# Inverse columns with weights of 128 rows by 64 columns, and ten transfers issued from three engines

## What is computed

```python
def _spectral_conv(x, w):
    B, Cin, H, W = x.shape
    x_ft = jnp.fft.rfft2(x, norm='ortho')
    out = jnp.einsum('bixy,ioxy->boxy', x_ft[:, :, :M1, :M2], w.astype(x_ft.dtype))
    out_ft = jnp.zeros((B, w.shape[1], H, W // 2 + 1), dtype=x_ft.dtype)
    out_ft = out_ft.at[:, :, :M1, :M2].set(out)
    return jnp.fft.irfft2(out_ft, s=(H, W), norm='ortho')
...
for sw, cw, cb in ((sw0, cw0, cb0), (sw1, cw1, cb1), (sw2, cw2, cb2), (sw3, cw3, cb3)):
    x1 = _spectral_conv(x, sw)
    x2 = jnp.einsum('bchw,oc->bohw', x, cw) + cb[None, :, None, None]
    x = _gelu(x1 + x2)
```

## Time and profile before

| | |
|---|---|
| median of the runs | 1113.42 us |
| profiled execution, its own time | 1119.4 us |
| its span, first to last instruction | 1117.5 us |
| TensorE busy | 1026.7 us, 92% |
| VectorE, ScalarE, GpSimd busy | 55%, 37%, 12% |
| mean granted TensorE clock | 0.975 of 2.4 GHz |
| inverse columns (L1296), 4096 matmuls | 267.6 us busy |
| inverse rows (L1264), idle until the first modes have landed | 6.9 us, 8 times |

### The profile page before, as it was taken

How to read it: one execution, slowest core, us unless ns; L and a number is a source line. 1 busy time by engine, 2 the same in 40 slices (tenths; PEclk the granted TensorE clock), 3 DMA queues, 4 the chain that set the end, 5 groups by cost and what they waited for, 6 DMA issues and landing times.

```text
span 1117.5 us, 36304 instructions
## 1 busy us (share of the span) xinstructions
PE 1026.7 (92%) x16860; PEld 655.4 (59%) x16860; DVE 618.3 (55%) x773; ACT 410.1 (37%) x554; POOL 137.2 (12%) x127
## 2 busy tenths in 40 slices
PE   4899999999989999999899899999999999689996
PEld 3577667667757633676577567667316788522221
DVE  2257457726833221477358347733153577769887
ACT  2332223223223486232232233223676777411100
POOL 6000000000000000000000000020010755334421
PEclk9999999999999999999999999999999899779999
DMA  5220130022022300310220130020001000000000
GB/s 189 90 75 4 47 100 22 4 90 75 4 76 73 94 6 21 111 41 3 90 76 3 53 96 21 3 91 17 4 22 43 2 2 1 1 1 1 1 10 10
DMA packets 25660, 46.75 MB, mean 42 GB/s; under 512 B 9437, under 2 KB 10488, under 8 KB 24869
## 3 DMA queue, kind: packets, MB, share of 16 engines
q1 hardware_dynamic: 24694, 43.49, 12.6%
q10 hardware_dynamic: 384, 0.66, 0.2%
q0 software_dynamic: 432, 0.29, 0.1%
HBM read 30.25 MB, written 10.89 MB: 37 GB/s over the span
## 4 chain that ended last, share of the span: by engine, by line
PE 73%; DVE 11%; issue 5%; ACT 4%; DMA 3%; SPq 2%; POOL 2%; ACTq 0%; POOLq 0%; DVEq 0%
PE PSALL L1296 23%; PE PSALL L1264 7%; PE PSALL L1159 5%; PE PSALL L1374 4%; PE PSALL L1287 4%; PE PSALL L1173 4%; PE PSALL L525 4%; PE PSALL L1240 3%; PE PSALL L1384 3%; DVE WORK L1504 3%; PE PSALL L428 3%; DMA WORK<-MIXED 2%; PE PSALL L513 2%; DVE WORK L1523 2%; PE PSALL L407 2%
## 5 line engine op out<-in xcount | busy, mean ns | idle before, releaser
L1523 DVE STREAM_TRANSPOSE WORK<-PSALL 128x1024 f32<-128x1024 f32 x128 | 152.4, 1229 | 277.4 <-PE PSALL L1264 277.4
L1296 PEld LDWEIGHTS PSALL<-EW,WORK 64*128 64x128 f32 x4096 | 251.2, 193 | 65.5 <-issue 48.3
L1296 PE MATMUL PSALL<-EW,WORK 64*128 64x128 f32 x4096 | 267.6, 284 | 12.8 <-DVE WORK L1523 12.8
L1424 ACT ACTIVATE X<-PSALL,TABLES 128x1024 f32<-128x1024 f32 x128 | 141.7, 1114 | 336.7 <-PE PSALL L1296 336.7
L1504 DVE STREAM_TRANSPOSE WORK<-PSALL 128x1024 f32<-128x1024 f32 x84 | 104.3, 1241 | 32.8 <-PE PSALL L1159 30.9
L1405 ACT COPY SPEC<-PSALL 128x400 f32<-128x400 f32 x64 | 54.0, 850 | 136.8 <-PE PSALL L1173 132.8
L1173 PEld LDWEIGHTS PSALL<-TABLES,WORK 128*64 128x64 f32 x2000 | 67.1, 138 | 48.6 <-DVE WORK L1504 31.4
L705 POOL MEMSET SW<- 64x4160 f32 x1 | 3.6, 3560 | 712.6 <-PE PSALL L1248 712.6
L1004 DVE TENSOR_TENSOR WORK<-PSALL,X 128x832 f32<-128x832 f32 x80 | 79.8, 1018 | 19.4 <-PE PSALL L513 17.9
L1173 PE MATMUL PSALL<-TABLES,WORK 128*64 128x64 f32 x2000 | 80.7, 228 | 7.8 <-DVE WORK L1504 3.8
L525 PE MATMUL PSALL<-WORK,SPEC 128*64 128x416 f32 x320 | 74.8, 549 | 0.0
(11 more groups left out here) (157 smaller groups left out, 1166.6 us busy)
## 6 DMA issues: line engine op xcount, KB each, us to landing
SW<-in_spec_w SPq DMA_DIRECT2D x160, 80.0 KB, 2.5
spec_scr<-MIXED SPq DMA_DIRECT2D x24, 400.0 KB, 3.3
SPEC<-spec_scr SPq DMA_DIRECT2D x32, 200.0 KB
WORK<-spec_scr SPq DMA_DIRECT2D x16, 200.0 KB
WORK<-MIXED SPq DMA_DIRECT2D x64, 40.0 KB
WORK<-in_coords_w SPq DMA_DIRECT2D x2, 1024.0 KB, 4.8
XC<-in_coords_c SPq DMA_DIRECT2D x2, 1024.0 KB, 7.2
hid_scr<-WORK SPq DMA_DIRECT2D x64, 8.0 KB
```

What stands on the lines that cost most here:

```text
L1296: m = pe.matmul(PS[2 * p + z][:, 2 * b * GRID:(2 * b + 2) * GRID], G[64 * z:64 * z + 64, n % 2, b, h:h + 4, :, c].rearrange("p q o -> p (q ...
L1424: nc.scalar.activation(X[:, n].rearrange("p b (z d) c w -> p d z b (c w)", z=2)[:, p, :, :, 2 * t * GRID:2 * (t + 1) * GRID], PSALL[:, 2 * ...
L1523: nc.vector.transpose(G[:, n % 2, 2 * x + y].rearrange("p h o v -> p o h v"), PSALL[:, 4 + 2 * x:6 + 2 * x, :].rearrange("p k (h o v) -> p ...
```

## The change

In `image_columns` one product now has 128 rows of G by 64 columns as weights; the two column tiles j (`tile_position` (0, 0) and (0, 64)) write the two halves of the partitions of one bank. EW becomes a block-diagonal table of 128 rows by 128 columns: the upper 64 rows hold the transform for the first 64 output columns and the lower ones for the other 64. So one product covers both c, and each region of PSUM is added to once instead of twice. The number of products, and the 128 columns that each streams, stay. The tables of the inverse rows are put into another order to match. The ten transfers are shared out anew: SyncE issues x = 0 of d = 0 to 3 and x = 1 of d = 4, ScalarE x = 0 of d = 4, and GpSimd x = 1 of d = 0 to 3 with a counter of its own, for which TensorE and VectorE wait too. `keep_busy` is called with 2 instead of 3.

```diff
         DW = sb("DW", [128, 2, 2 * Q])
-        EW = sb("EW", [128, 3 * GRID])
+        EW = sb("EW", [128, 2 * GRID])
         ident = sb("ident", [128, 128])
...
         stored = [Count(sem(f"modes_stored{g}"), 1, unit=16) for g in range(NG)]
-        straight_in = Count(sem("first_modes_copied"), 1, unit=16 * 2 * KXD)
+        straight_in = Count(sem("first_modes_copied"), 1, unit=16 * (KXD + 1))
+        pool_straight_in = Count(sem("first_modes_copied_by_pool"), 1, unit=16 * (KXD - 1))
         loaded = [None] + [Count(sem(f"modes_loaded{g}"), 1, unit=32) for g in range(1, NG)]
...
-        def straight(eng, d, x):
+        def straight(eng, d, x, count):
...
                           MIXED[NG * x:128:2 * NG, d * MODES * CH:(d + 1) * MODES * CH]
-                          ).then_inc(straight_in.sem, 16)
+                          ).then_inc(count.sem, 16)
...
                     turn.wait(mix_ready, -(-(d + 1) * KYG // 4))
-                    for x in range(2):
-                        straight(sp, d, x)
+                    straight(sp, d, 0, straight_in)
                 turn.wait(mix_ready, N_MIX)
+                straight(sp, KXD - 1, 1, straight_in)
                 for n in range(1, NG):
...
                     turn.wait(straight_in, 1)
+                    turn.wait(pool_straight_in, 1)
                 elif y == 0:
...
-                for c in range(2):
-                    h = 4 * (2 * p + t)
-                    for z in range(2):
-                        m = pe.matmul(PS[2 * p + z][:, 2 * b * GRID:(2 * b + 2) * GRID],
-                                      G[64 * z:64 * z + 64, n % 2, b, h:h + 4, :, c].rearrange("p q o -> p (q o)"),
-                                      EW[64 * z:64 * z + 64, (1 - c) * GRID:(3 - c) * GRID],
-                                      start=False, stop=True, skip_group_check=True, tile_position=(64 * z, 0))
+                for z in range(2):
+                    for j in range(2):
+                        h = 4 * (2 * z + p) + 2 * j
+                        m = pe.matmul(PS[2 * p + z][64 * j:64 * j + 64, 2 * b * GRID:(2 * b + 2) * GRID],
+                                      G[:, n % 2, b, h:h + 2, :, t].rearrange("p q o -> p (q o)"), EW[:],
+                                      start=False, stop=True, skip_group_check=True, tile_position=(0, 64 * j))
                 return m
...
                 pointwise(l, 0, 0)
-                keep_busy(3)
+                keep_busy(2)
                 inverse_rows(l, 0, 0)
...
                     act.wait_ge(ho_out.sem, p * ho_out.stride)
-                for x in range(2):
-                    straight(act, KXD - 1, x)
+                straight(act, KXD - 1, 0, straight_in)
...
                         turn.wait(straight_in, 1)
+                        turn.wait(pool_straight_in, 1)
                         for g in range(1, NG):
...
                 pool.dma_start(dst[:], src).then_inc(tail_w, 16)
+
+            turn = Steps(pool)
+            for p in range(PASSES):
+                for l in range(LAYERS):
+                    if l == 0 and p:
+                        pool.wait_ge(ho_out.sem, p * ho_out.stride)
+                    for d in range(KXD - 1):
+                        turn.wait(mix_ready, -(-(d + 1) * KYG // 4))
+                        straight(pool, d, 1, pool_straight_in)
+                    turn.next()
             tail_pool(pool)
...
     twice = np.where(k == 0, 1.0, 2.0)[:, None]
-    idft_w = np.zeros((2, RI, Q, GRID))
-    idft_w[:, 0, 0:MODES], idft_w[:, 1, 0:MODES] = twice * cos.T, -twice * sin.T
+    idft_w = np.zeros((2, RI, Q, 2, GRID))
+    for c in range(2):
+        idft_w[c, 0, 0:MODES, c], idft_w[c, 1, 0:MODES, c] = twice * cos.T, -twice * sin.T
...
         forward = np.array(forward).reshape(2, Q)
-        inverse = [row_of(l, 2 * half + p, q, 2 * t + c)
-                   for half in range(2) for p in range(2) for t in range(SETS) for q in range(4) for c in range(2)]
+        inverse = [row_of(l, p, q, 2 * t + c)
+                   for c in range(2) for p in range(4) for q in range(4) for t in range(SETS)]
         inverse = np.array(inverse).reshape(2, Q)
...
         "outside": 1 - band, "band4": np.tile(band * f(HD ** -0.5), (1, 4)),
-        "idft_w": np.pad(idft_w.reshape(128, GRID), ((0, 0), (GRID, GRID))).astype(f), "ident": np.eye(128, dtype=f),
+        "idft_w": idft_w.reshape(128, 2 * GRID).astype(f), "ident": np.eye(128, dtype=f),
     }
```

## The result

The changed kernel takes 1089.12 us, median of four runs (1086.85 to 1089.77), beside 1114.89 us for the kernel before; the ratio is 0.9771, with a 95% interval of 0.9746 to 0.9796. It is 2.3% faster. The forecast was 1084.5 us, between 1077 and 1096: sign and range held, the number was 4.6 us too low. The profiled execution of the changed kernel took 1089.02 us (span 1086.0), like its median; that of the kernel before had taken 1119.4, 4.5 us over its own median of four runs.

A forecast was written before the change was run, and what follows sets the result against it. TensorE, busy 92% of the span, was taken as the bound, with inverse columns and WORK<-MIXED transfers on the chain. Gains of 16 + 11 + 1.6 = 29 us took 1119.4 to 1090.5, at the median 1084.5 us; range 1077 to 1096.

The forecast's parts named there:

- What paces the columns: Inverse columns: 128-column loads set 118 ns a pair; with 64-column loads the stream sets it, about 109.5 ns.
- rival 3: Inverse columns: a load cannot run under a stream using its rows; 162 ns a pair, 1187 us in all; 3%.
- Rival 1: Inverse columns: loads go on setting the pace at 118 ns a pair; gain 16 us, 1097.5 us; 8%.
- rival 4: Table or row order makes transposes or waits other than read; no change, 1113 us; 2%.
- Part 1: Inverse columns with weights of 128 rows by 64 columns: stretches get shorter, 16 us gained, 3 to 20 between bounds.
- Part 2: Transfers before the inverse rows, one filler less: rows start 3.0 us after last copy, not 4.37; 11 us gained.
- Part 3: Inverse stages of layers 0 and 4: less idle time may remove drops to 1.2 GHz; 1.6 us, 0 to 3.2.
- The sum: Whole kernel: 16 + 11 + 1.6 = 29 us off profiled 1119.4 gives 1090.5; 6 us less for the median, 1084.5.

The follow-up runs named there:

- half stream: Kernel before, weights of 64 rows by 128 columns kept, each product streaming only the 64 table columns that are not zero: 1125.83 us, ratio 1.0109.
- columns alone: Changed kernel with the old transfers and keep_busy(3), so only the new weights of the inverse columns remain: 1099.93 us, ratio 0.9864.
- transfers alone: Changed kernel with the old weights of 64 rows by 128 columns and the old table: 1104.26 us, ratio 0.9905.
- without GpSimd: Changed kernel with GpSimd's four transfers given back to SyncE, which then issues nine: 1106.39 us, ratio 0.9910.
- second execution of before: Kernel before, unchanged, profiled a second time: 1111.93 us, span 1110.1.
- second comparison: Changed kernel, unchanged, measured again beside a version with one block of the t = 0 columns moved later: 1087.61 us, ratio 0.9772.

## Why the prediction was right, and where its number was off

- **What paces the columns: right.** The half stream shows that the old stream did not set the pace (118 ns as before), and the change gave 109 ns a pair (109.5 forecast). That the stream of 107 ns paces the new columns was forecast and fits, but no run changed it there. This decides rival 3 as well: the load under a stream through the same rows costs no 162 ns. The rule of the Trainium skill that it rested on (TensorE: Matmul & The Clock Gate, section Part 3: Packing small matmuls - row/col tiling: a load overlaps only where its row group differs) does not hold for these column tiles, which share all 128 rows at 109 ns a pair. Rival 1 (118 ns) is out too, and rival 4 (other waits than were read): the stretches have the lengths and the one wait that were forecast.
- **Part 1, 16 us: right.** From the first to the last matmul's start, a stretch with t = 1 fell from 3.76 to 3.445 us, 0.316 x 32 = 10.1; with t = 0 from 3.83 to 3.62, 0.21 x 24 = 5.1; n = 0 gave 0.11 a layer, 0.9. Sum 16.1, and the stages show 16.2. Alone it measured 15.2 us by the ratio, with an interval of 10.6 to 19.7; the medians lie 15.8 apart.
- **Part 2, 11 us: the mechanism right, the size that of one execution.** The rows start 2.95 us after the copy (3.0 forecast), with 0.33 us of idle time a layer (0.35 forecast), GpSimd's transfers land first, and one filler call less costs nothing. But the 4.37 us of before were the mean of an execution with late issues: in the second it is 4.17, so that the change is worth 8 x 1.22 = 9.7 us there, and the two other traces with the old transfers (columns alone, half stream) show 4.06 and 4.04. The transfers alone, with the clock's part, measured 10.6 us by the ratio (7.1 to 13.9) where 12.6 had been put on them. The Trainium skill says of issuing from several engines (DMA: Bandwidth & Descriptors, section Issuing engines are not separate DMA queues) that it saves only the sequencer's time to issue, usually small beside the transfer. The trace agrees on what is saved, and shows that it need not be small: 0.6 us an issue, nine of them on one queue, cost 10 us without GpSimd, and more through the clock.
- **Part 3, 1.6 us: right in size, by luck.** The 1.6 was the middle of 0 to 3.2, and not one drop of two foreseen. Between the first two profiled executions both drops went (3.2 us); the second execution of before, like the run with the columns alone, has only layer 0's, which makes 1.6.
- **The sum: where the number went off.** 29 us, taken from the profiled 1119.4, gave 1090.5; the changed kernel's profiled execution took 1089.02. Then the forecast took the difference of 6 us between profiled execution and median off the result, as if profiling added it to any kernel. It does not, as the second executions of both kernels show. Of the 7.4 us that the first execution took longer than the second one, 4.0 lie in the start and the tail, which the change leaves as they are; but 1.7 are later inverse rows, which the change removes, and the 11 us of part 2 had counted them already. (Another 1.6 are layer 4's clock, and part 3 had counted one drop of the two.) Made against the second execution, the sum is 16 + 9.7 + 1.6 = 27.3 us. And the base was low: three executions gave 1113.42, all 35 give 1114.7. From that, 27.3 less is 1087.4; the ten executions of the changed kernel in its two comparisons have a median of 1087.9. So of the 4.6 us some 1.3 lie in the base and 1.6 in the sum, mostly part 2; the other 1.7 are no more than the scatter of a median of four (1089.12 here, 1087.61 in the second comparison).

Not settled: what makes SyncE's issues late in one execution and not in the next. From layer to layer SyncE's last issue starts 0.71 to 2.57 us after the copy in the first execution (over 1.1 us in four layers) and 0.72 to 1.67 in the second (over 1.1 us in three); in layer 0 of both it is ScalarE's second issue that starts last, 1.58 us after the copy, behind a first one of 1.5 us. Single issues take up to 1.6 us instead of 0.6, and the traces do not show what they waited for. The changed kernel starts its last issue at 0.03 us in nearly all layers, so it has less of this to lose.

## What to carry to other kernels

Divide a long stretch by its count and hold the quotient against both the load and the stream: where the load is the longer one, weights of fewer columns on two column tiles pay even though the matmuls stay as many. Count how many transfers one queue issues after the last release; three queues are worth it where something waits for the last of them, and filler is needed only as far as it keeps the idle time short, and one execution is not enough to see how far that is. A sum worked out against one profiled execution must be carried to the median as a difference of causes: what was slow in that execution may be just what the change removes, and then it can't be taken off twice.

## What the runs showed of the hardware that was not expected

- ScalarE's single issue in layer 0 takes 1.47 us, for 0.62 in layer 1, and yet the rows behind it start 2.91 us after it, no later than the 2.88 in layer 1. What the queue shows as issuing is not all ahead of the transfer:

```profile
35.08 1.47 ACTq L325 DMA_DIRECT2D WORK<-MIXED  x1
...
37.99 1.31 PE L1266 MATMUL PSALL<-WORK,TABLES 64*64 64x512 f32 x16 [0.28 <-issue]
```

- GpSimd issues a transfer of 40 KB in 0.56 us, as fast as SyncE (0.6), and its transfers landed 1.6 to 2.7 us after the last copy although its last one started 0.72 us before it (by the updates of its counter in the changed kernel's trace).
- In one execution with one filler call, idle time of 1.1 to 1.4 us before the inverse rows left the clock at 2.4 GHz in eight layers of eight; in one without any, 2.1 to 2.6 us brought it to 1.2 GHz in eight of eight. In the kernel without GpSimd 1.27 us came before a drop and 1.74 us before none, so the length alone does not decide. And halving the streams under the same loads brought the clock down with TensorE busy all the time.
